# A ViT tower on one core: new instruction orders on TensorE, ScalarE, VectorE and GpSimd in the embedding and attention stages

## The reference

```python
h = _L0_tok_ref(x, ln_gamma, ln_beta, w, b)          # 5 shifted images, 16x16 patches, LayerNorm over 3840, @ w (3840x192) + b
h = h + _L0_attn_ref(_layernorm(h), qkv_w, qkv_b, out_w, out_b)   # mask: keys j % 8 == 0 with j <= i, j == i, j == i-1
h = h + _L0_ffn_ref(_layernorm(h), router_w, w1, b1, w2, b2)      # 8 experts of 768, the two largest gates

# in _L0_ffn_ref
for e in range(E):
    w_e = jnp.sum(top_w * (top_i == e), axis=-1)[:, None]
    h = jax.nn.gelu(flat @ w1[e] + b1[e], approximate=False)
    out = out + w_e * (h @ w2[e] + b2[e])
```

## Time and profile before

| | |
|---|---|
| median of 3 runs | 186.98 us |
| profiled execution, its own time | 187.43 us |
| its span, from the first to the last instruction | 185.7 us |
| outside the span | 1.73 us |
| PE busy | 174.2 us, 94% |
| VectorE (DVE) busy | 137.6 us, 74% |
| ScalarE (ACT) busy | 116.8 us, 63% |
| GpSimd (POOL) busy | 83.8 us, 45% |

### The profile page before, as it was taken

One profiled execution on the slowest core, in us unless ns is written; L12 is line 12 of the kernel. 1 busy time (PEld: TensorE's weight loads), 2 busy tenths in 40 slices (PEclk: granted clock), 3 DMA queues, 4 the chain that ended last, 5 costly groups with the idle time before them and its releaser, 6 DMA issues.

```text
span 185.7 us, 3462 instructions
## 1 busy us (share of the span) xinstructions
PE 174.2 (94%) x1131; PEld 149.1 (80%) x1131; DVE 137.6 (74%) x311; ACT 116.8 (63%) x208; POOL 83.8 (45%) x111
## 2 busy tenths in 40 slices
PE   5898999979989979899999999999999999999994
PEld 2485768869767658689899899899899999999994
DVE  5379994887349883997788688688688688687553
ACT  2499553844625355757777776776876875973730
POOL 7867401251897334920651652652652662560000
PEclk9999999978999999999999999999999999999999
DMA  5999999600105920046005505405405400000002
GB/s 112 245 287 286 243 203 247 132 2 0 45 24 170 260 59 0 0 129 169 4 0 145 151 0 153 143 2 161 136 0 155 141 2 0 0 4 0 0 0 85
DMA packets 14979, 18.08 MB, mean 97 GB/s; under 512 B 2467, under 2 KB 10776, under 8 KB 14966
## 3 DMA queue, kind: packets, MB, share of 16 engines
q1 hardware_dynamic: 14422, 17.90, 37.5%
q10 hardware_dynamic: 544, 0.03, 0.2%
HBM read 17.14 MB, written 0.39 MB: 94 GB/s over the span
## 4 chain that ended last, share of the span: by engine, by line
PE 78%; DVE 11%; issue 3%; DMA 3%; ACT 2%; SPq 1%; POOL 0%; DVEq 0%
PE ps L372 32%; PE ps L1190 17%; PE ps L1192 8%; DMA early<-in_x 3%; PE ps L878 2%; DVE big_r L1271 2%; DVE merge L1336 2%; PE ps L1029 2%; PE ps L384 2%; PE ps L1240 1%; PE ps L996 1%; PE ps L1239 1%; PE ps L1238 1%; PE ps L1059 1%; PE ps L379 1%
## 5 line engine op out<-in xcount | busy, mean ns | idle before, releaser
L372 PE MATMUL ps<-big_r,wsplit 128*128 128x512 f32 (+1 forms) x245 | 61.5, 387 | 0.0
L794 ACT ACTIVATE early<-ps,b1t 128x512 f32<-128x512 f32 x48 | 32.8, 684 | 29.1 <-PE ps L372 27.4
L1190 PE MATMUL ps<-wsplit,big_r 128*128 128x384 f32 x168 | 49.7, 355 | 0.7 <-DVE big_r L1271 0.7
L1271 DVE TENSOR_TENSOR big_r<-early,big_r 128x512 fp32r<-128x512 f32 x48 | 35.9, 751 | 15.8 <-ACT big_r L335 15.3
L372 PEld LDWEIGHTS ps<-big_r,wsplit 128*128 128x128 f32 x245 | 42.0, 189 | 6.3
L1192 PE MATMUL ps<-wsplit,big_r 128*128 128x192 f32 x168 | 42.1, 250 | 0.0
L1190 PEld LDWEIGHTS ps<-wsplit,big_r 128*128 128x128 f32 x168 | 31.5, 188 | 2.7 <-issue 1.1
L1192 PEld LDWEIGHTS ps<-wsplit,big_r 128*128 128x128 f32 x168 | 32.0, 190 | 1.3
L335 ACT ACTIVATE big_r<-early 128x512 fp32r<-128x512 f32 x48 | 30.3, 632 | 1.5
L1609 DVE SCALAR_TENSOR_TENSOR merge<-sq,gates,merge 128x192 f32<-128x192 f32 x32 | 26.9, 866 | 0.0
L317 POOL TENSOR_TENSOR wsplit<-stage,wsplit 128x768 fp32r<-128x768 f32 x4 | 7.4, 1844 | 19.7 <-ACT wsplit L335 15.7
(11 more groups left out here) (241 smaller groups left out, 283.5 us busy)
## 6 DMA issues: line engine op xcount, KB each, us to landing
stage<-in_L_ffn_w SPq DMA_DIRECT2D x4, 576.0 KB, 6.7
early<-in_L_ffn_w SPq DMA_DIRECT2D x4, 576.0 KB, 5.8
shifted<-in_L_tok_w SPq DMA_DIRECT2D x6, 288.0 KB, 7.9
early<-in_x SPq DMA_DIRECT2D x6, 256.0 KB, 5.2
stage<-in_L_ffn_w SPq DMA_DIRECT2D x4, 384.0 KB, 4.3
stage<-in_L_ffn_w SPq DMA_DIRECT2D x8, 192.0 KB, 5.3
early<-in_L_ffn_w SPq DMA_DIRECT2D x4, 384.0 KB, 3.3
early<-in_L_ffn_w SPq DMA_DIRECT2D x8, 192.0 KB, 4.3
```

The lines of the kernel that those rows point to most:

```text
L372: mm = nc.tensor.matmul(dst, lhs, rhs, start=(first and n == 0), stop=(last and n == 4))
L794: nc.scalar.activation(gf[:, j % NG], ps[:, HPB[j % 4], :], ACT.Gelu, bias=b1t[:, bass.ds(k, 1)]).then_inc(s_gelu, 1)
L1190: nc.tensor.matmul(ps[:, AB[t], 0:2 * D], g_hi[:, j % NG, tok], w2c, start=(f == 0), stop=False)
L1271: return nc.vector.tensor_tensor(o, a, b, op)
```

## The change

On TensorE the first half's tiles of every chunk go ahead of the second half's; the sums of squares go ahead of chunk 2, groups 0 and 1 of the small weights behind the spreading, group 2 behind all chunks, group 3 behind the transposes of n1's first half; two matmuls without use (`IDLE`) go. ScalarE follows in the same sense. In attention TensorE's `repeated_v(0)` goes ahead of `near_by_heads(1)` and `transposed_p(1)` ahead of `repeated_v(3)`; VectorE's `scores(1)` goes ahead of `denominators(0)`; GpSimd makes the low part of expert 0's layer two behind `near_values` of both halves. Ahead of the experts VectorE makes `low_hidden(0, 0)` ahead of `two_largest`.

```diff
@@ gpsimd
             split_low_w1(pool, 0, 0)
-            split_low_w2(pool, 0, 0)
...
                 near_values(g)
             pool.wait_ge(s_nv, G)
+            split_low_w2(pool, 0, 0)
             rstd(1, 0)
@@ scalar
+            act.wait_ge(s_sumsq, 1)
+            copy(sq_part, ps[:, SQB, :]).then_inc(s_sqpart, 1)
             merged_high(1, 0)
             merged_high(1, 1)
+            act.wait_ge(s_beta, 1)
+            copy(beta_part, ps[:, BETAB, 0:D]).then_inc(s_betapart, 1)
...
             split_high(0, 0)
             split_high(0, 1)
-            small_high(3)
-            copy(b1t[:], ps[:, WB[3], 400:400 + E * FC]).then_inc(s_wathi, 1)
...
             high_parts(0, s_nt, NTB, nt, s_nhi)
+            small_high(3)
+            copy(b1t[:], ps[:, WB[3], 400:400 + E * FC]).then_inc(s_wathi, 1)
             split_high(0, 2)
@@ tensor
-            chunk(2 * C - 1, (0, 1))
+            pe.wait_ge(s_wdup, 2)
+            small_transposes(0)
+            small_transposes(1)
...
+            chunk(2 * C, HALF0)
+            chunk(2 * C + 1, HALF0)
+            chunk(2 * C - 1, HALF0)
+            for ch in ORDER[1:]:
+                chunk(ch, HALF1)
             pe.wait_ge(s_watlo, 2)
             small_transposes(2)
-            chunk(2 * C, (2, 3))
-            chunk(2 * C + 1, (2, 3))
-            chunk(2 * C - 1, (2, 3))
-            pe.wait_ge(s_watlo, 1)
-            small_transposes(3)
...
             masks(1)
-            for _ in range(IDLE):
-                nc.tensor.matmul(ps[:, NTB[0], :], xh[:, 0, 0:P], xh[:, 0, :], start=True, stop=True)
             transposes(0, n1, s_n, lambda t: t + 1, NTB, s_nt, s_ndup)
+            small_transposes(3)
...
             strided_scores(1)
+            repeated_v(0)
             near_by_heads(1)
-            repeated_v(0)
             repeated_v(1)
...
             repeated_v(2)
+            transposed_p(1)
             repeated_v(3)
-            transposed_p(1)
@@ vector
+            scores(1)
             denominators(0)
-            scores(1)
...
+            low_hidden(0, 0)
             two_largest()
-            low_hidden(0, 0)
             low_hidden(0, 1)
```

More of the change, by code:

```diff
@@ L265, in vit_tower @@
         EARLY = 3
-        IDLE = 2
         LAG = 3
@@ L691, in _ @@
                  ones_f[0:HALO, 0:4].rearrange("p (k n) -> p k n", k=2)).then_inc(s_mw, 1)
+            act.wait_ge(s_sumsq, 1)
+            copy(sq_part, ps[:, SQB, :]).then_inc(s_sqpart, 1)
             merged_high(1, 0)
             merged_high(1, 1)
+            act.wait_ge(s_beta, 1)
+            copy(beta_part, ps[:, BETAB, 0:D]).then_inc(s_betapart, 1)
+            act.wait_ge(s_merge, MERGES.index("halo 1") + 1)
+            copy(wlmh[0:HALO, 2 * C:NX, HIGH0:], wm_halo[0:HALO]).then_inc(s_whi, 1)
             act.wait_ge(d_small, 16 * SMALL_DMAS)
@@ L696, in _ @@
             copy(wraw[0:E, 8, D:], wraw[0:E, 8, P:D]).then_inc(s_wdup, 1)
-            act.wait_ge(s_sumsq, 1)
-            copy(sq_part, ps[:, SQB, :]).then_inc(s_sqpart, 1)
-            act.wait_ge(s_merge, MERGES.index("halo 1") + 1)
-            copy(wlmh[0:HALO, 2 * C:NX, HIGH0:], wm_halo[0:HALO]).then_inc(s_whi, 1)
             merged_high(1, 2)
-            small_high(0)
-            small_high(1)
-            act.wait_ge(s_beta, 1)
-            copy(beta_part, ps[:, BETAB, 0:D]).then_inc(s_betapart, 1)
             act.wait_ge(s_beta, 2)
@@ L709, in _ @@
                                  scale=1.0 / FEAT).then_inc(s_meansq, 1)
+            small_high(0)
+            small_high(1)
             act.wait_ge(s_mask, 2)
@@ L928, in _ @@
             pe.wait_ge(s_xlo, 4)
-            chunk(0)
-            chunk(1)
+            HALF0, HALF1 = (0, 1), (2, 3)
+            chunk(0, HALF0)
+            chunk(1, HALF0)
             beta_products(1, (2, 3, 4))
+            pe.wait_ge(s_m, 1)
             pe.wait_ge(s_xhi, XGROUPS)
             pe.wait_ge(s_xlo, XGROUPS)
-            chunk(2)
-            pe.wait_ge(s_m, 1)
             pe.wait_ge(s_xsq, XGROUPS)
@@ L948, in _ @@
             mm.then_inc(s_sumsq, 1)
-            chunk(3)
-            chunk(4)
-            pe.wait_ge(s_wdup, 2)
-            small_transposes(0)
-            small_transposes(1)
-            pe.wait_ge(s_sqpart, 1)
+            chunk(2, HALF0)
             pe.wait_ge(s_gb, 2)
@@ L961, in _ @@
             beta_product(band[0:1, BAND0 - 1:BAND0 + 1], tokb_row[:]).then_inc(s_beta, 1)
-            pe.wait_ge(s_hhi, 1)
-            pe.wait_ge(s_hlo, 1)
-            pe.wait_ge(s_mw, 2)
-            chunk(2 * C, (0, 1))
-            chunk(2 * C + 1, (0, 1))
+            chunk(0, HALF1)
+            chunk(3, HALF0)
+            chunk(4, HALF0)
             pe.wait_ge(s_first, 1)
@@ L972, in _ @@
                                  start=True, stop=True)
+            pe.wait_ge(s_sqpart, 1)
             for t in range(TT):
@@ L976, in _ @@
             mm.then_inc(s_beta, 1)
-            chunk(2 * C - 1, (0, 1))
+            pe.wait_ge(s_wdup, 2)
+            small_transposes(0)
+            small_transposes(1)
+            pe.wait_ge(s_hhi, 1)
+            pe.wait_ge(s_hlo, 1)
+            pe.wait_ge(s_mw, 2)
+            chunk(2 * C, HALF0)
[3 more added lines that the diff above has]
+                chunk(ch, HALF1)
             pe.wait_ge(s_watlo, 2)
             small_transposes(2)
-            chunk(2 * C, (2, 3))
-            chunk(2 * C + 1, (2, 3))
-            chunk(2 * C - 1, (2, 3))
-            pe.wait_ge(s_watlo, 1)
-            small_transposes(3)
             def transposes(g, src, ready, count, banks, done, again=None):
```

## The result

The changed kernel took 188.16 us, the median of four executions (187.84 to 190.35), beside 186.94 (186.33 to 187.38) for the kernel before on the same chip: a ratio of 1.0101 [1.0064, 1.0138], slower. Measured again later, in six executions: 188.81 (187.98 to 190.71), ratio 1.0125 [1.0084, 1.0167]. The forecast was 189.2 in a range of 187.2 to 191.0.

What follows compares the result with a forecast made beforehand. Experts' stage bound by PE's own work from 76.5 us; ahead of it the limit passes between engines. +1.4 (embedding's +0.2 included) and +0.8 make +2.2 on the median 186.98: 189.2 us, range 187.2 to 191.0.

Steps and rivals of the forecast that it cites:

- Embedding: Embedding, n1's first half: 2.5 us gained at the head all lost in ScalarE's queue, and 0.2 more: +0.2 us.
- Attention up to the near values: Attention: second half's scores 0.75 us sooner, GpSimd's near values end at 61.5 in place of 62.14; 0.7 us gained.
- The multiplication behind L330: Attention: merge<-raw,rden, two SBUF inputs, is held by GpSimd's split_low_w2(0) and ends at 64.8; not held, near 62.55.
- +1.4 at transposes(1): Attention's term, with the embedding's +0.2 in it: the held multiplication turns a gain of 0.7 us into a loss.
- Start of the experts: Experts' start: low_hidden(0, 0) held by GpSimd, layer two 0.17 us later, PE stalls at slice 2: +0.8, at most +1.05.
- the forecast's alternative: Experts' start: instead of the cast, the second one-hot with two SBUF inputs is caught by GpSimd's long instruction.
- Rival 1: Attention: PE's clock falls once more while VectorE is held, adding 1 to 1.7 us: 190.5; chance 0.18.
- Rival 2: Attention: one lock fails, the multiplication slips in ahead of GpSimd's long instruction; -0.85 + 0.8: 186.9; chance 0.09.
- rival 3: merge<-raw,rden and low_hidden(0, 0): nothing held for long, the long rows having another cause; -0.85 and -0.5: 185.6; chance 0.12.
- Rival 4: Embedding: the low clock at 41 us goes or halves, -1.7 at most: 187.5 to 188.3; chance 0.11.

Runs made afterwards that it cites:

- emb_only: The kernel before with only the change's embedding edits (TensorE's and ScalarE's new orders, IDLE gone): 186.61 us, ratio 1.0007.
- act_alone: The changed kernel with ScalarE's splits of the experts' weights moved later, behind the copy of n1's last columns: 187.42 us, ratio 1.0025.
- u_head: The changed kernel with VectorE's two_largest ahead of low_hidden(0, 0) again: 188.02 us, ratio 1.006.
- only_w2: The kernel before with one edit, GpSimd's low part of expert 0's layer two behind both halves' near values: 189.99 us, ratio 1.0166.
- halves: The changed kernel with GpSimd's low part of expert 0's layer two cut into two instructions, a semaphore wait between: 187.06 us, ratio 1.0029.
- all_new: The changed kernel with the edits of act_alone and new_head together: 184.87 us, ratio 0.991, leaving out one execution of 569.01 us.
- u_both_act: u_both with act_alone's edit (ScalarE's weight splits later), nothing else: 184.62 us, ratio 0.9895.
- u_both: The changed kernel with GpSimd's low part of expert 0's layer two early again and two_largest ahead of low_hidden(0, 0) again: 186.40 us, ratio 0.9977.
- new_head: between, with GpSimd's low parts of expert 1's w1 and w2 later and low_hidden(0, 2) ahead of the indices: 186.82 us, ratio 1.0018.
- between: The changed kernel with GpSimd's low part of expert 0's layer two between the two halves' near values: 187.31 us, ratio 1.0027.

## Why the prediction was right, and which terms were off

The direction and the mechanism stood: two GpSimd instructions in new places held VectorE, and PE waited. The sum was too large by half of itself in the traces, +2.2 against +1.07, and by 0.1 to 1.0 in the two sets' medians (+2.06 and +1.22). That the second comes so near is in part luck: its kernel before had the high clock in 18 of 29 executions, which no term of the sum had in it.

- **Embedding, +0.2 forecast, between -0.3 and +0.6; -0.54 in the changed kernel's trace, -0.37 in emb_only's: wrong in sign, and the largest miss.** The statistics came 2.6 us earlier on the copy's count, and ScalarE's queue did take most of it, as act_alone shows by taking the queue away. But ScalarE could start at 34.18, 34.84 in before's time, not 35.35: I had put PE's end of chunks and transposes too late. And the queue was 2.44 us, not 2.57. So norm<-norm began at 37.28 of before's time, not 37.9. By medians the gain is hardly there (emb_only is 0.14 below before), and in its trace a third of it is gone by layer two (0.25).
- **Attention up to the near values: about right.** The forecast had their end at 61.5 in place of 62.14, -0.64 with the embedding's +0.2 in it, so -0.84 without. The trace has it at 59.93, on the copy's count 1.55 earlier than before, and without the embedding's 0.54 that is -1.01.
- **The multiplication behind L330: right, the hold too large.** I reckoned 64.8 - 62.55 = 2.25 us. The trace has 2.25 - 0.56 = 1.69, and the medians 1.62. The addition in front began 0.30 us behind the near values' end (59.93 to 60.23), so that less of L330 was left, and the multiplication ended 0.42 behind L330, not 0.6. Together with the two terms above, the forecast's +1.4 at transposes(1) became +0.33.
- **Start of the experts, +0.8: right.** On the copy's count +1.01 at slice 2, where transposes(1) had brought +0.33: +0.68; the medians give 0.66. low_hidden(0, 0) was held to 75.91 and PE waited for the copy of the logits. The cast went ahead of L330 and the second one-hot was caught, the forecast's alternative, with the same wait of 0.70.
- **Rival 1**, the second fall, is shown by two traces, u_head's and act_alone's, behind waits of 1.82 and 1.81 us; those of the changed kernel have none behind 1.81, nor has only_w2's behind 1.99. It was priced at 1 to 1.7 us and costs 0.8 to 1.1. Its 190.5 was met by two of ten executions (190.35 and 190.71), but the one such execution that was profiled, of u_head, owes more to a longer first fall, which no rival had. It was no rival but a spread above the forecast. **Rival 2** and **rival 3** are excluded by the held rows, rival 3's even share also by halves. The Trainium skill's rule (SBUF — State Buffer, section "SBUF: two separate sides"), a lock for a whole instruction, agrees with halves: 1.04 against 2.25 us for the same bytes. **Rival 4** did not happen in any of the ten executions. In act_alone, all_new and u_both_act the low clock near 40 us did go, together with ScalarE's wait, but it was worth less than the 1.7 us it was priced at: 0.34 between the traces of u_both and u_both_act, and 0.6 to 0.9 between before's own executions.
- What I hadn't seen is that the embedding's orders were good and only ScalarE's was in the way. On the copy's count u_both_act brings nt's first product 2.04 us earlier than before and near_by_heads(1) 2.34. Against u_both it is 1.47 at the first and 1.81 at the second, the size of the wait of 1.52 and some tenths of the low clock. I had written that the gain is "lost in ScalarE's queue" and didn't go on to price the queue.

The record also tells most of u_both_act's 1.8 us against u_both apart. Four of u_both's twelve executions have a mean clock of 0.998 or more, and took 185.83 to 186.58, no less than its four at 0.991 (185.85 to 186.33). The traces say the same: 1.47 us are there at the first product, and only 0.34 come in the stretch in which u_both's clock is low. So it is mainly the wait, which also holds up VectorE's statistics of the second half behind nt's low part. And u_both's medians show half of the gain of its trace (-0.55 against -1.22 at the end) because they mix the clocks: at 0.991, as in both traces, u_both's median is 185.93 and before's 187.26, -1.33; at 0.998 or more the two are at 186.32. Why u_both gains nothing there is not settled, with four executions of it.

## What to carry to other kernels

Before a long GpSimd instruction is moved, list the VectorE instructions with two SBUF inputs that come up within its time: here each ended only behind it (2.25 us in place of 0.56). Put it under VectorE work that reads PSUM, or cut it (1.04). Where a reordering brings work forward and the gain stops in another engine's queue, price that queue as the next edit: here a few moved lines on ScalarE turned a change of -0.55 us (u_both) into one of -2.0. Align two traces by an event that the change can't touch before you subtract them. Where a kernel's executions fall into groups by their mean clock, compare like groups, and say how many executions each has.

## What the runs showed of the hardware

- The hold is per instruction: VectorE gets in between two GpSimd instructions, with a wait for a semaphore between them (halves, 1.04 against 2.25 us) or without (merge<-halo,rden, 0.80 us), and the second of them is then longer (1.61 and 1.19 us). It also hits tiny ones: the two one-hots of 32 elements took 2.79 us, against 0.42 when free.
- A cast of 32 elements took 0.18, 1.15 or 2.36 us, by where GpSimd's long subtraction lay; under GpSimd's power, a row of 1.30 us, it took 0.18. The index searches ahead of it took 0.15 or 0.16 each, also under the subtraction.
- The same wait of 1.8 us is followed by the low clock in some traces (u_head, act_alone) and not in others (the changed kernel's two), and a low stretch near 40 us lasted 3.4 us in some and over 6 us in others (u_head, new_head). Before, two waits of 0.70 and 0.78 us close together were followed by it in about half of the executions; in u_both_act and all_new, with no wait of more than 0.77 us from n1's first transposes to the experts, the mean clock was at least 0.997 in all twelve executions. The longest wait alone doesn't decide.
- The arrival of the first transfers varies by up to 0.95 us: the copy of the last pixels began at 9.92 us (after) to 10.87 (between) in the profiled executions.
